# Attention layers of a graph network: the largest neighbour score from TensorE sums of powers of two in place of a running maximum on VectorE

## The reference, cut to what matters

```python
h = x @ W
e = (h @ a_src)[src] + (h @ a_dst)[dst]
e = jnp.where(e > 0, e, 0.2 * e)
m = jax.ops.segment_max(e, dst, num_segments=n)
ex = jnp.exp(e - m[dst])
s = jax.ops.segment_sum(ex, dst, num_segments=n)
out = jax.ops.segment_sum((ex / (s[dst] + 1e-16))[:, None] * h[src], dst, num_segments=n) + b
```

## Time and profile before

| | us |
|---|---|
| median of three runs | 2177.43 |
| lowest, highest | 2173.3, 2178.93 |
| profiled execution, its span | 2175.7 |
| PE busy in the span | 1732.0 (80%) |
| DVE busy | 1688.5 (78%) |
| ACT busy | 1225.4 (56%) |
| POOL busy | 1110.4 (51%) |
| attention, first exponent to the last product | 1324 to 2025 |

### The profile page before, as it was taken

How to read it: one execution, slowest core, us unless ns; L and a number is a source line. 1 busy time by engine, 2 the same in 40 slices (tenths; PEclk the granted TensorE clock), 3 DMA queues, 4 the chain that set the end, 5 groups by cost and what they waited for, 6 DMA issues and landing times. The chain is left out here.

```text
span 2175.7 us, 34765 instructions
## 1 busy us (share of the span) xinstructions
PE 1732.0 (80%) x8596; PEld 850.5 (39%) x8597; DVE 1688.5 (78%) x4278; ACT 1225.4 (56%) x2361; POOL 1110.4 (51%) x982
## 2 busy tenths in 40 slices
PE   2777776883898989999999867889778995889676
PEld 0222222551444444444444453444333442333344
DVE  6999997435677777777777659998899979998554
ACT  5777776212444444444444414899379964999311
POOL 1000000005777777777777703789368873789400
PEclk9999999896999999999999955999679996999878
DMA  6000000102111111111111230000000000000000
GB/s 174 0 0 0 0 0 9 65 4 64 38 34 39 34 38 34 38 34 38 34 39 33 44 99 0 1 1 1 1 1 0 1 1 0 1 0 1 15 1 15
DMA packets 29627, 50.60 MB, mean 23 GB/s; under 512 B 12821, under 2 KB 13827, under 8 KB 29055
## 3 DMA queue, kind: packets, MB, share of 16 engines
q0 software_dynamic: 17664, 18.12, 4.8%
q1 hardware_dynamic: 11890, 31.59, 4.7%
HBM read 36.58 MB, written 7.39 MB: 20 GB/s over the span
## 5 line engine op out<-in xcount | busy, mean ns | idle before, releaser
L800 POOL DMA_INDIRECT adj<-h_table,l_idx x544 | 569.9, 1048 | 166.4 <-issue 158.2
L1563 POOL TENSOR_TENSOR gat_ring<-gat_ring,adj 125x750 f32<-125x750 f32 (+2 forms) x375 | 503.2, 1347 | 203.5 <-ACT gat_ring L1628 198.2
L990 DVE TENSOR_SCALAR adj<-adj,node_key 125x1024 f16<-125x1024 f16 x825 | 380.0, 503 | 202.4 <-PE psum L935 180.3
L935 PE MATMUL psum<-adj,x_sb 125*128 125x512 f16 x1650 | 400.4, 387 | 0.4 <-DVE adj L990 0.4
L1462 DVE SCALAR_TENSOR_TENSOR gat_ring<-x_sb,gat_node,psum 125x750 f32<-125x750 f32 (+2 forms) x375 | 316.8, 856 | 19.5 <-ACT x_sb L1590 9.5
L1625 ACT ACTIVATE gat_ring<-gat_ring,gat_node 125x750 f32<-125x750 f32 (+2 forms) x339 | 278.8, 822 | 67.6 <-DVE gat_ring L1462 64.0
L1701 PE MATMUL psum<-gat_ring,gat_hx 125*65 125x500 f32 (+1 forms) x500 | 266.0, 627 | 53.5 <-POOL gat_ring L1563 51.2
L378 PE MATMUL psum<-col_hot,src_hot 128*128 128x500 bf16 x808 | 205.6, 376 | 111.2 <-DVE src_hot L307 90.7
L863 ACT ACTIVATE l_z<-psum 128x320 f32<-128x320 f32 x204 | 89.2, 437 | 346.0 <-PE psum L914 345.8
L1430 DVE SCALAR_TENSOR_TENSOR psum<-adj,gat_node,psum 125x750 f32<-125x750 f16 (+1 forms) x276 | 257.0, 931 | 1.3
L1628 ACT ACTIVATE gat_ring<-gat_ring 125x750 f32<-125x750 f32 (+2 forms) x339 | 249.5, 736 | 10.7
(11 more groups left out here) (246 smaller groups left out, 2058.0 us busy)
## 6 DMA issues: line engine op xcount, KB each, us to landing
adj<-h_table,l_idx POOLq DMA_INDIRECT x544, 2.5
adj<-key_table SPq DMA_DIRECT2D x33, 250.0 KB
adj<-adj SPq DMA_DIRECT2D x3, 1662.5 KB
adj_saved<-adj SPq DMA_DIRECT2D x1, 3840.3 KB
adj<-adj_saved SPq DMA_DIRECT2D x5, 688.2 KB
x_sb<-in_x SPq DMA_DIRECT2D x1, 781.2 KB
x_saved<-x_sb SPq DMA_DIRECT2D x1, 781.2 KB
out<-x_sb SPq DMA_DIRECT2D x5, 156.2 KB
```

The source lines that it names most:

```text
L800: pool.indirect_dma_start(out=to[:, t, :], out_offset=None, in_=table[:, :], in_offset=bass.IndirectOffsetOnAxis(ap=index[:, t:t + 1], axi ...
L935: last = pe.matmul(psum[:, PAIR[half] + t, :], h_parts[:, k, :], select[0:P, k % SELECTS, t * GE:(t + 1) * GE], start=(k == 0), stop=(k == ...
L990: v.tensor_scalar(select[0:P, k % SELECTS, :], keys, node_key[:, k:k + 1], None, ALU.is_equal).then_inc(s_sel, 1)
L1563: pool.tensor_tensor(slot, slot, adj[:, k, cols(c)], ALU.mult).then_inc(s["weight_ready"], 1)
```

## The change

The running maximum is gone (`first_max`, `max_step`, `max_transposes`), and so are the `degree` matmuls and the copies of their results by ACT. In their place, once per layer, DVE turns each source's score into 63 powers of two, one for each of 63 windows of the score's range, by writing the bits of bf16 numbers (`codes` in the tile `levels`, [125, 25 x 64] bf16; the 64th column holds ones). For each destination tile PE adds up, over the 25 source tiles, counts times levels: `level_sum`, a matmul with 128 columns of adj (fp16) as the weights and the 64 columns of `levels[:, k, :]` as the moving operand. Read as integers, the 63 fp32 sums give their exponents; clamped and added over the windows they give an upper bound of the largest neighbour's score (`node_step` 0 to 2). The 64th sum is the degree, which DVE copies out in layer 0.

The 75 level sums of chunk 0 run on PE at the layer's start. Those of chunk 1 (150) are spread over PE's first 17 products, 8 or 9 behind each; those of chunks 2, 3 and 4 (150, 150, 100) over 25 products each, six, six and four behind each. `node_step` 0 stays behind exponent 19 of a chunk and now waits for all level sums of the next one. DVE also takes over the clamp of every fourth step in chunks 0 to 3 (before only every second one of chunk 4).

```diff
     def bounded_by_dve(c, k):
-        return c == GC - 1 and k % 2 == 1
+        return k % 2 == 1 if c == GC - 1 else k % 4 == 3
...
             def shifts(layer, link):
...
+                link(v.scalar_tensor_tensor(offsets, a_unit.unsqueeze(2).to_broadcast([P, NT, WINDOWS]),
+                                            float(WINDOWS * WINDOW_BITS * BF16_STEP),
+                                            starts[:, :].unsqueeze(1).to_broadcast([P, NT, WINDOWS]), ALU.mult, ALU.add))
+                v.tensor_scalar(codes, offsets, 0.0, float((LOW_BIT + WINDOW_BITS) * BF16_STEP), ALU.max, ALU.min)\
+                    .then_inc(s["levels_ready"], 1)
...
                 if i == 0:
-                    op = v.tensor_reduce(m, in_psum(sums_of(g), g % GC), AX.X, ALU.max)
+                    op = v.tensor_scalar(mine, level_sums_of(g)[:, :, 0:WINDOWS].bitcast(I32), LOW_CODE, HIGH_CODE, ALU.max, ALU.min)
                 elif i == 1:
-                    op = v.tensor_scalar(m, m, -0.5, ext[:, 4:5], ALU.add, ALU.mult)
+                    op = v.tensor_reduce(m, mine, AX.X, ALU.add)
...
-            def max_transposes(g):
+            def level_sum(g, i):
                 c = g % GC
...
+                at = (GSTART[c] + t) * P
+                op = pe.matmul(level_sums_of(g, 128)[:, t, :], b["adj_all"][0:P, k, at:at + 128], levels[:, k, :],
+                               start=(k == 0), stop=(k == NT - 1), skip_group_check=True)
...
-                if DEG_EARLY + c < len(deg_tiles[layer]):
-                    degree(psum[0:P, sums_of(g) + 1, 0:1], deg_tiles[layer][DEG_EARLY + c])
...
+                        n = c * NT + k + 1
+                        if n <= SUMMED_AT:
+                            target = -(-GCHUNK[1] * NT * n // SUMMED_AT)
+                        else:
+                            whole, part = divmod(n - SUMMED_AT, NT)
+                            target = NT * sum(GCHUNK[1:2 + whole]) + part * sum(GCHUNK[2 + whole:3 + whole])
+                        while taken < min(target, len(coming)):
+                            level_sum(*coming[taken])
+                            taken += 1
```

More of the change, by code:

```diff
@@ L1225, in attention @@
 def attention(nc, sem, b):
-    adj, psum, ident, x_sb, x_flat, aggT, vecs, deg, stat, ring, hT, asd, node, rr, ext, wx, ones16 = (b[k] for k in (
-        "adj", "psum", "ident", "x_sb", "x_flat", "aggT", "vecs", "deg", "stat", "ring", "hT", "asd", "node", "rr", "ext", "wx",
-        "ones16"))
+    adj, psum, ident, x_sb, x_flat, aggT, vecs, deg, stat, ring, hT, asd, node, rr, ext, wx = (b[k] for k in (
+        "adj", "psum", "ident", "x_sb", "x_flat", "aggT", "vecs", "deg", "stat", "ring", "hT", "asd", "node", "rr", "ext", "wx"))
+    levels, starts_i, starts = b["levels"], b["starts_i"], b["starts"]
+    codes = levels[:, :, 0:WINDOWS].bitcast(mybir.dt.int16)
     over_features = b["over_features"]
-    a_unit, k_s, m_max, m_log, neg_a_s, rsum = (node[:, k, :] for k in range(6))
+    a_unit, k_s, bits, m_log, neg_a_s, rsum, a_base = (node[:, k, :] for k in range(7))
     feats = b["feats"]
@@ L1236, in attention @@
     oT = hT[:, :, :].rearrange("p a b -> p (a b)")[:, 0:GWIDE]
-    mxs, rrow = x_flat[:, 0:GWIDE], x_flat[:, GWIDE:2 * GWIDE]
+    clipped, rrow = x_flat[:, 0:max(GCHUNK) * WINDOWS].rearrange("p (t j) -> p t j", j=WINDOWS), x_flat[:, GWIDE:2 * GWIDE]
+    offsets = ring_flat[:, 0:NT * WINDOWS].rearrange("p (t j) -> p t j", j=WINDOWS)
     LAYERS, STEPS = 3, GC * NT
-    MAX, ROW1 = 4, 6
-    START, CATCH_UP, LEAD = 3, 17, 8
-    PROJECT_AT, ABSORB_AT, TRANSPOSE_AT, NODE_AT = 6, 11, 14, 20
+    ROW1 = 6
+    PROJECT_AT, ABSORB_AT, SUMMED_AT, NODE_AT = 6, 11, 17, 20
     WXC = D + 3
-    DEG_EARLY = 5
-    deg_tiles = [[t for t in range(NT) if t % LAYERS == l] for l in range(LAYERS)]
-    assert all(len(d) - DEG_EARLY <= GC - 1 for d in deg_tiles)
     row_parts = (slice(0, EVEN), slice(EVEN, P))
@@ L1270, in bounded_by_dve, with bounded_to, level_sums_of @@
     def bounded_by_dve(c, k):
-        return c == GC - 1 and k % 2 == 1
+        return k % 2 == 1 if c == GC - 1 else k % 4 == 3
+    def bounded_to(g, k):
+        return sum(bounded_by_dve(i // NT % GC, i % NT) for i in range(g * NT + k + 1))
+    def level_sums_of(g, rows=P):
+        return psum[0:rows, 4 + g % 2, 0:GCHUNK[g % GC] * LEVELS].rearrange("p (t j) -> p t j", j=LEVELS)
     def pair(bank, rows=P):
@@ L1324, in _ @@
             v = nc.vector
-            done = 0
             def add_aggregate():
@@ L1381, in shifts @@
             def shifts(layer, link):
+                dve.wait_ge(s["starts"], 2)
                 a_s = asd[:, layer % 2, 0, :]
@@ L1433, in node_step, with degrees_in @@
+                link(v.tensor_scalar(a_base, asd[:, layer % 2, 1, :], ext[:, 7:8], None, ALU.add))
+            def degrees_in(g):
+                sums = level_sums_of(g)[:, :, WINDOWS]
+                v.tensor_scalar(deg[:, tiles_of(g)], sums, -1.0, None, ALU.add).then_inc(s["degrees_read"], 1)
             def node_step(g, i):
                 tiles, a_d = tiles_of(g % GC), asd[:, (g // GC) % 2, 1, :]
-                m, log, ad, r1, r2 = m_max[:, tiles], m_log[:, tiles], a_d[:, tiles], rr[:, 0, tiles], rr[:, 1, tiles]
+                m, log, ad, r1, r2 = bits[:, tiles], m_log[:, tiles], a_d[:, tiles], rr[:, 0, tiles], rr[:, 1, tiles]
+                mine = clipped[:, 0:GCHUNK[g % GC], :]
@@ L1452, in node_step @@
                 op.then_inc(s["node_rows"], 1)
+                if i == 0 and g < GC:
+                    degrees_in(g)
             def exponent(g, k):
@@ L1494, in _ @@
             layer_norm(add_aggregate())
+            dve.wait_ge(s["starts"], 1)
+            v.tensor_copy(starts[:, :], starts_i[:, :]).then_inc(s["starts"], 1)
             weight_columns(1)
@@ L1505, in _ @@
                 shifts(layer, link)
-                first_max(layer)
+                if layer == 0:
+                    dve.wait_ge(s["x_kept"], 32)
                 for i in range(6):
                     node_step(first, i)
-                steps = [(first + c, k) for c in range(1, GC) for k in range(NT)]
-                taken = 0
-                while taken < START:
-                    max_step(*steps[taken])
-                    taken += 1
                 for c in range(GC):
@@ L1636, in _ @@
         def _(pe):
-            def degree(to, t):
-                for k in range(NT):
-                    last = pe.matmul(to, adj[:, k, t * P:(t + 1) * P], ones16[:, 0:1],
-                                     start=(k == 0), stop=(k == NT - 1), skip_group_check=True)
-                return last
             def aggregate_back(c):
@@ L1736, in _ @@
                 first = layer * GC
-                if layer > 0:
-                    pe.wait_ge(s["exponent_ready"], first * NT)
-                for i in range(DEG_EARLY):
-                    last = degree(psum[0:P, ROW1, i:i + 1], deg_tiles[layer][i])
-                last.then_inc(s["degrees_summed"], 1)
-                max_transposes(first)
+                for i in range(GCHUNK[0] * NT):
+                    level_sum(first, i)
                 row2(first)
                 row1(first)
+                coming = [(first + c, i) for c in range(1, GC) for i in range(GCHUNK[c] * NT)]
+                taken = 0
                 for c in range(GC):
```

130 lines of the change are left out of this document (41 added, 89 removed).

## The result

| | before | after |
|---|---|---|
| median, four runs each | 2177.66 | **2074.2** (2072.31 to 2075.87) |
| ratio, 95% interval | | 0.9522 (0.951 to 0.9534) |
| span of the profiled execution | 2175.7 | 2074.0 |
| PE busy | 1732.0 (80%) | 1681.0 (81%) |
| DVE busy | 1688.5 (78%) | 1490.4 (72%) |

A forecast was written before the change was run, and what follows sets the result against it. DVE was taken as the bound in stretches 0 to 2. Savings of 20.6 us in layer 0 and 18.3 in each other layer, 57.2 in all, took 2175.7 to 2118.5; the median lies 1.7 above: 2120, range 2088 to 2160.

The forecast's parts named there:

- DVE's and ACT's part: Attention chunks: without most maximum steps DVE falls to about 40 us a stretch, off the path; ACT below 40 too.
- POOL's part: Chunks of 750: steps of 1.64 give a floor of 41.0; six clamps at 0.3 add 1.8, floor 42.8 us.
- PE's part: Matmuls in the chunks, said to decide: 0.057 us a level sum, so a step of 750 holds PE for 1.66 us.
- Stretch 0: First exponent of chunk 0 to that of chunk 1: 33.9 us against 43.4, -9.5, including 3.0 for products at 1.2 GHz.
- Stretches 1 to 3: From chunk 1's first exponent to chunk 4's: 45.0, 46.0 and 43.0 us, changes of -3.3, -1.0 and -0.9.
- Layer start: Before a layer's first exponent: offsets, codes, 75 level sums and a clamp take 10.2 us in place of 14.6; -4.5 in all.
- Last stretch: From chunk 4's first exponent on: the same work, 25 degrees fewer in layer 0, -1.4 us.
- The new wait: `node_step` 0 waits some 3 us for level sums; the ring holds 5 us of PE work, so PE does not run dry.
- Sums nearly free: Rival: a level sum costs 0.03, POOL is then the bound; 9.8 us a layer less, 2091; chance 0.12.
- Clamps and POOL shut each other out: Rival: POOL stands still for whole DVE clamps, 0.9 each and not 0.3; +6.8 us a layer, 2141; chance 0.12.
- Dearer pairs: Rival: level sums between products cost 0.081 each, loads and streams mixed; +9.6 us a layer, 2149; chance 0.08.
- PE at 1.2 GHz: Rival: level sums keep the clock low and cost 0.1075 each; 24 us a layer, 2192, slower; chance 0.08.

The follow-up runs named there:

- the wide run: The changed kernel with 128 moving columns in each level sum in place of 64: 2237.91 us, ratio 0.9651.

## Why the prediction was right and wrong

**What bounds the kernel: right.** DVE's 0.91 a step was the bound of stretches 0 to 2, and its removal paid there most.

**DVE's and ACT's part: right.** DVE has 33 to 35 of 42.5 us in a chunk of 750, ACT 37 to 38; "about 40" and "below 40" were forecast. The clamp of 750 took 1.02 in the mean, from 0.61 to 1.92; 0.72 to 2.1 was forecast.

**POOL's part: near in the number, by luck in part.** The floor of 42.8 was worked out from 41.0 and 1.8. Measured are 42.4 a stretch (127.3 / 3), less than the floor: POOL is busy for 38.4 to 40.0 of that and idle for 3.1 in the mean (28.1 / 9), mostly at the seams between chunks. The 1.64 was read from five steps in a row that were all of the long kind, where the mean over all was 1.574; the waits made up for it.

**PE's part: this step failed.** "The two agree although their streams differ by 127 columns, so I take 0.057." They agree by accident. The degrees were 125 weight columns and one moving one: 0.056 was their weight load, as the run with 125 columns shows (0.0544 with 64 moving columns). The eight pairs were 128 and 128: 0.057 was their stream, as the wide run shows (0.0556). A level sum has neither, 128 weight columns that load fast and a stream of 64. Two rows that agree while everything in them differs don't speak of a common cause; each should have been asked what limits it, and the sum takes the larger of load and stream for its own shape. In that form, the 128 by 128 row bounds a load of 128 columns from above (no more than 0.057), and the sum's lower end, half of it, was as well founded as the middle. The Trainium skill, TensorE: Matmul & The Clock Gate, "Weight-path perf modes — Fast Weight Load (FWL) and DoubleRow", has the rule: a faster weight load is on when there are exactly 128 weights and they are not fp32. By it the degrees could not stand for a level sum; the runs agree, 0.029 with 128 and 0.0544 with 125. I had not weighed it.

Of the 50.6 us in attention that the forecast missed, 38 hang on this price, by the run with 125 weight columns. Term by term:

- *Stretch 0*, 33.9 forecast: 29.6 in layer 0, 27.7 in the others. The price is 4 us of it (150 x 0.028). With the price alone layer 0 would have been at 29.7. There three products came at a granted clock of 0.50, the first two of them 1.8 us ahead of the next, until it rose at 1328.20. Layers 1 and 2 are 2 us shorter for two reasons. The first product comes 2.9 us behind the first exponent and not 4.2 (1529.53 less 1526.60), since ACT's table load of 1.28 us between the first Relu and the first Exp is there in layer 0 alone; I had taken 4.2 for all. And only two products come at 0.50 before the clock rises at 1533.0. The 3.0 that I added for them was too much: counted from the starts of the products it is 2.2 us in layer 0 and 1.6 in layer 1.
- *Stretches 1 to 3*, 45.0, 46.0 and 43.0 forecast: 42.5, 42.7, 42.1. PE's step is 1.47 and not 1.66 (six sums are 0.16 less, the changes between groups 0.03 less), and POOL's mean step 1.62 and not 1.71 with its share of clamps, so the 1.0 to 2.2 for two engines so close that they do not both run full did not come.
- *Layer start*, -4.5: -8.2. The 75 sums took 3.6, not 6.4 (2.8 us); from the reduction to the first exponent it is 1.2 us quicker, of which I had forecast only the tiny instruction; the codes over 1575 elements took the full 1.80, not 1.5.
- *Last stretch*: -1.4 in layer 0 forecast. With the start of the next layer it is -11.2 and -9.4 where -5.9 and -4.5 were forecast; in layer 2, with no start behind it, -0.4. So chunk 4 itself hardly moved, and what was gained lies in the start.

**The new wait: right in its effect.** It costs DVE 15 us over 12 chunks outside the starts, 1.2 each where I had expected 3, and taking it away gained nothing.

**The rivals.** *Sums nearly free* (0.03, 2091) had the mechanism: PE under POOL, the stretches of 750 near POOL's floor (though in the second of them PE stayed the fuller, 41.44 us against 39.97). It still fell short by 17 us, since it had 29.9 for stretch 0 in every layer where 27.7 came in two of them, 43.6 a stretch of 750 where 42.4 came, and only 2 us less at the start. I gave it 0.12, because "one column took no less than 128"; that sentence compared a load with a stream. *Clamps and POOL shut each other out* (0.9 a clamp) is refuted as a price: POOL's step grows from 1.574 to 1.624 with one clamp to four steps, 0.2 a clamp. The collisions are there all the same: 38 of the 225 steps took more than 1.73 us, the longest of the kernel before, 1.86 in the mean where the others kept 1.576; and DVE's clamp of 750, 0.61 at its shortest, is stretched to 1.02 in the mean (1.20 where DVE clamps every second step). By the rule that I cited from the Trainium skill, SBUF — State Buffer, "Who interferes with whom", POOL would have stood still for the whole clamp wherever the clamp came first. These runs do not show that: a POOL step that is hit is some 0.3 longer, half of the shortest clamp. *Dearer pairs* at 0.081 is refuted too: neither 0.029 nor, with the wide stream, 0.0556 is near it. *PE at 1.2 GHz*: a level sum at half clock does not cost 0.1075 but 0.056, nine in 0.50 us at 1324.85; 75 in 3.6 us at a mean of 0.62 granted are 0.048. With 125 weight columns the 0.107 does come back, but only where 0.50 was granted: in the starts and at the first products of chunk 0. The granted clock in the attention layers was 0.95 to 0.99, above the 0.86 and 0.88 of before.

**The range** ended at 2088 because all cases but one had 0.057 or more. Both ends of a price that no row shows belong in the range with their full effect: at 0.03 a PE step is 1.50, so the stretches of 750 go to POOL's 42.8 (1.8 us less a layer than the rival's 43.6, 43.6 and 43.0), and 75 sums at the start give 4.1 and not 2: 4 a layer in all, 12, and the rival would have stood at 2079. Part of that nearness is luck too, as the 42.8 was no floor.
